# A cross-attention kernel on one core: new memory map of the opening, normalisation on ScalarE, Wo stores behind product stores

## The chip, the cores and the metric

The kernel runs on one core of a Trainium2 chip. The metric is the device time of one execution in microseconds (us); the time of a kernel is the median of its runs. Engines: PE is TensorE (matmuls), DVE is VectorE, ACT is ScalarE, POOL is GpSimd, SP is SyncE, which here issues all DMAs. SBUF has 128 partitions; addresses below are KiB within a partition. PSUM has eight banks of 128x512 f32.

## The reference

```python
a = layer_norm(ctx, gamma, beta)                 # ctx: 8 x 64 x 1024
Q = x @ Wq.T                                     # x: 8 x 1024 x 1024, 16 heads of 64
K = a @ Wk.T ; V = a @ Wv.T
attn = softmax(Q K^T / 8, masked)                # per head, 64 keys
out = x + tanh(gate) * (attn V) @ Wo.T
```

All in float32.

## The kernel before

**Algebra.** Scores are not made from Q. For each batch b the kernel first makes M[b] = Wq^T K[b]^T (1024 x 1024: model dimension by 16 heads x 64 keys), so that the scores of a batch are x[b] @ M[b]. The output is (attn V) @ Wo^T, so the main loop is 32 products of 512 x 1024 by 1024 x 1024: rounds n = 0 to 15 (scores, two a batch, with M[b]) and n = 16 to 31 (output, with Wo). Each product is made by Strassen's scheme in Winograd's form: seven half-size products, in the order P1, P5, P6, P3, P7, P2, P4. Every product of the seven is a step s = 7n + k (224 steps), of two items g = 0, 1, each four groups of three matmuls: every f32 operand is split into a high part (rounded to fp32r) and a low part, and high x high, high x low and low x high are summed. A step lasts 5.44 us on PE.

**Per step.** The left operand (a quarter of x, or a sum of quarters that `sum_a` makes in `a_sum`) is split by ACT (`split_a_hi`) and DVE (`split_a_lo`) into `a_ring`. The right operands are split once a batch into `parts` (seven regions of 16 KiB at 0 to 112) by `split_b_hi` on ACT and `split_b_lo` on DVE, in 14 half pieces q (q // 2 is the product, 0 = P1, 1 = P5, 2 = P6, 3 = P3, 4 = P7, 5 = P2, 6 = P4); `sum_b` (DVE) makes the sums in `b_raw` between them, counted by `t_made`. `refill_step` says behind which step a piece is split; -1 is ahead of step 0. P1, P5, P6 and P4 of a scores round are first uses and are copied out by ACT, the others are added to `c_out` by DVE (`add_out`), and `store_quad` stores them. PE's `item` waits for these splits, copies and adds. P5, P3 and P2 share two banks, so the P2 step waits for the add of P3.

**The opening.** SP loads four tiles of the context, the constants (gamma, beta, gate, mask, on one semaphore `consts_in`), 16 weight items (`load_weight`, 256 KB), then x. DVE takes statistics of each tile, POOL the reciprocal root (`rstd`), DVE normalises (L777), PE transposes (L1030), DVE scales by gamma and beta, ACT and DVE split. ACT splits the high part of a weight item (`split_weight_hi`, L622), POOL the low one (L574). Then PE makes 48 items in a written-out order (`OPS`): K in 16, M in 16 (`m_pair`), V in 16, with the M items interleaved with K and V. M item i (half, c) gives 128 rows of M for all batches: ACT and DVE copy alternate banks to `m_stage` (three buffers), `store_m` stores them. Batch 0's parts go directly to `b_raw` (L389, L391; the last four, on `b22_in`, are the second quadrant pair), the others to DRAM scratch. V is split in `v_out` and stored by `store_v`.

**Order.** Every engine works its own queue in program order, and SP its DMA queue. ACT ahead of step 0: weight splits, M copies, then `refills(-1)` (q 0 to 3), `split_a_hi(0)`, the four V splits. DVE: the same for its side, with `sum_b` behind each `split_b_lo`. SP: after all items it waits for `m_stored[1]` and `b22_in[1]`, since x pair 1 lies in a stage buffer, loads x(1), stores V, loads x(2); then `slot(z)` for each half step: product stores (`after_product`), x loads, Wo quarter loads, Wo stores, M loads, x quads and softmax loads.

**Wo.** During the first scores rounds the Wo matrix is read in quarters, summed (`sum_wo`), split (`round_wo` on ACT, `split_wo_lo` on DVE) into `wo_ring` of three slots, and stored to DRAM scratch in 56 pieces (`store_wo_split`, L364), to be loaded as `parts` later. ACT waits before a piece until the store of three pieces earlier has landed.

## Time and profile before

| | |
|---|---|
| median of 3 runs | 1564.25 us (1563.99 to 1564.56) |
| profiled execution, its time | 1560.93 us |
| its span (first to last instruction) | 1559.2 us |
| PE busy | 1531.3 us (98%), 7104 matmuls |
| DVE busy | 1128.9 us (72%) |
| ACT busy | 872.8 us (56%) |
| POOL busy | 356.1 us (23%) |
| DMA | 289.77 MB, mean 186 GB/s |
| chain that ended last | PE 90%, DMA 4%, DVE 3% |

Starts are us from the span's start. A PE record of 0.39 us is one 128x512 matmul in a pipeline: successive ones start 0.227 us apart. A timeline row is start, duration, engine, line, operation, output<-input, count, and in brackets how long the engine had been idle before it and what released it.

### The profile page before, as it was taken

Reading aid. Unit: us, or ns where it says so; the run is one execution under the profiler, and the core shown is the slowest. Engines: PE = TensorE matmul, PEld = TensorE weight load, DVE = VectorE, ACT = ScalarE, POOL = GpSimd, SP = SyncE. Lnnn points to the kernel's source line nnn. Section 1 sums busy time; section 2 is a strip of 40 time slices with the busy share of each in tenths; the row PEclk is TensorE's granted clock in tenths of the full one; section 3 lists DMA queues with packets and bytes.
Section 4 is the critical chain, followed back from the end, with each engine's and each line's share of the span. In section 5 each row is a group of like instructions: output and inputs, shape, how many; then the busy total and the mean of one; then the engine's idle time right before and its main releaser. Section 6 shows DMA issues by size and latency. Waiting matters only on the chain.

```text
span 1559.2 us, 20380 instructions
## 1 busy us (share of the span) xinstructions
PE 1531.3 (98%) x7104; PEld 1245.8 (80%) x7104; DVE 1128.9 (72%) x1356; ACT 872.8 (56%) x1874; POOL 356.1 (23%) x254
## 2 busy tenths in 40 slices
PE   7999899999999999999999999999999999999998
PEld 5666778888888888887887888888888888888887
DVE  6445888787878787879857777777777777777643
ACT  3556445454545454547766666666666666666521
POOL 5333000000000000001233344432344333444320
PEclk9999999999999999999999999999999999999999
DMA  7799765656565656556689344553445533445321
GB/s 251 222 364 392 275 215 178 210 202 222 178 220 187 211 182 216 190 188 184 202 292 294 115 136 142 157 157 114 125 125 168 169 123 120 123 145 167 109 93 69
DMA packets 225077, 289.77 MB, mean 186 GB/s; under 512 B 28240, under 2 KB 112336, under 8 KB 224976
## 3 DMA queue, kind: packets, MB, share of 16 engines
q1 hardware_dynamic: 224976, 288.48, 56.6%
q8 instruction: 57, 0.93, 0.2%
q14 instruction: 44, 0.36, 0.1%
HBM read 168.89 MB, written 116.39 MB: 183 GB/s over the span
## 4 chain that ended last, share of the span: by engine, by line
PE 90%; DMA 4%; DVE 3%; issue 1%; SPq 1%; ACT 0%; POOL 0%; DVEq 0%; ACTq 0%
PE banks L1036 28%; PE banks L1038 28%; PE banks L1037 28%; PE banks L1104 4%; PE banks L1065 3%; DMA wo_split_scratch<-wo_ring 1%; DMA xq<-x_t 1%; DMA m_scratch<-m_stage 1%; DVE parts L878 1%; DMA s_scratch<-c_out 1%; DVE a_sum L939 1%; DVE a_ring L872 1%; ACT a_ring L684 0%; PE banks L1160 0%; DMA c_out<-x 0%
## 5 line engine op out<-in xcount | busy, mean ns | idle before, releaser
L1036 PE MATMUL banks<-parts,a_ring 128*128 128x512 f32 x1792 | 711.6, 397 | 5.8 <-DVE a_ring L872 3.6
L1038 PE MATMUL banks<-parts,a_ring 128*128 128x512 f32 x1792 | 700.1, 391 | 0.0
L1037 PE MATMUL banks<-parts,a_ring 128*128 128x512 f32 x1792 | 698.9, 390 | 0.0
L1036 PEld LDWEIGHTS banks<-parts,a_ring 128*128 128x128 f32 x1792 | 336.9, 188 | 75.3 <-DVE a_ring L872 5.9
L1038 PEld LDWEIGHTS banks<-parts,a_ring 128*128 128x128 f32 x1792 | 336.8, 188 | 72.2
L1037 PEld LDWEIGHTS banks<-parts,a_ring 128*128 128x128 f32 x1792 | 337.4, 188 | 66.7
L961 DVE TENSOR_TENSOR c_out<-banks,c_out 128x1024 f32<-128x1024 f32 x160 | 195.5, 1222 | 147.9 <-PE banks L1038 142.6
L732 ACT ACTIVATE probs<-probs,neg_max 128x64 f32<-128x64 f32 x1024 | 259.1, 342 | 1.7 <-DVE neg_max L966 1.7
L684 ACT CAST a_ring<-a_sum 128x1024 fp32r<-128x1024 f32 x128 | 134.3, 1049 | 219.4 <-PE banks L1038 199.6
L597 POOL TENSOR_TENSOR probs<-probs,row_rec 128x512 f32<-128x512 f32 x128 | 134.5, 1051 | 479.7 <-DVE row_rec L975 479.7
L872 DVE TENSOR_TENSOR a_ring<-a_sum,a_ring 128x1024 fp32r<-128x1024 f32 x128 | 180.3, 1409 | 79.4 <-ACT a_ring L684 79.4
L684 ACT CAST a_ring<-xq 128x1024 fp32r<-128x1024 f32 x96 | 100.9, 1051 | 179.0 <-PE banks L1038 178.1
L872 DVE TENSOR_TENSOR a_ring<-xq,a_ring 128x1024 fp32r<-128x1024 f32 x96 | 117.9, 1228 | 52.1 <-ACT a_ring L684 52.1
L878 DVE TENSOR_TENSOR parts<-b_raw,parts 128x1024 fp32r<-128x1024 f32 x112 | 135.3, 1215 | 0.7 <-ACT parts L707 0.7
L607 POOL MEMSET v_diag<- 128x2048 f32 x1 | 1.8, 1821 | 566.8 <-DVE parts L878 566.8
L707 ACT CAST parts<-b_raw 128x1024 fp32r<-128x1024 f32 x112 | 114.1, 1048 | 9.6 <-DVE b_raw L898 5.2
L749 ACT COPY xq<-banks 128x512 f32<-128x512 f32 x128 | 75.2, 588 | 78.4 <-PE banks L1038 75.4
L979 DVE TENSOR_TENSOR p_parts<-banks,p_parts 128x512 fp32r<-128x512 f32 x128 | 86.2, 673 | 38.1 <-ACT p_parts L741 38.1
L741 ACT CAST p_parts<-banks 128x512 fp32r<-128x512 f32 x128 | 74.2, 580 | 67.1 <-PE banks L1104 66.8
L966 DVE TENSOR_REDUCE neg_max<-probs 128x8 f32<-128x512 f32 x128 | 83.7, 665 | 6.9 <-ACT probs L732 6.9
L844 DVE COPY m_stage<-banks 128x512 f32<-128x512 f32 x64 | 43.7, 690 | 60.4 <-PE banks L1065 48.0
L971 DVE TENSOR_REDUCE row_sum<-probs 128x8 f32<-128x512 f32 x128 | 86.4, 675 | 0.0
(75 smaller groups left out, 1354.4 us busy)
## 6 DMA issues: line engine op xcount, KB each, us to landing
xq<-x_t SPq DMA_DIRECT2D x32, 1024.0 KB, 6.8
s_scratch<-c_out SPq DMA_DIRECT2D x64, 512.0 KB, 3.1
probs<-s_scratch SPq DMA_DIRECT2D x128, 256.0 KB, 4.0
c_out<-x SPq DMA_DIRECT2D x64, 512.0 KB, 4.5
out<-c_out SPq DMA_DIRECT2D x64, 512.0 KB, 3.1
b_raw<-m_scratch SPq DMA_DIRECT2D x29, 1024.0 KB, 6.7
m_scratch<-m_stage SPq DMA_DIRECT2D x16, 1792.0 KB, 13.9
wo_split_scratch<-wo_ring SPq DMA_DIRECT2D x56, 256.0 KB, 5.7
```

The costliest lines, as they stand in the source:

```text
L597: nc.gpsimd.tensor_tensor(pr, pr, rec, ALU.mult).then_inc(probs_done, 1)
L684: nc.scalar.copy(a_ring[:, s % 2, 0], a_source(n, k)).then_inc(a_hi_made, 1)
L707: nc.scalar.copy(parts[:, k, 0, c:c + 2, :], b_raw[:, B_HOME[k], c:c + 2, :]).then_inc(b_hi_made, 1)
L732: last = nc.scalar.activation(prob(u)[:, cols], prob(u)[:, cols], ACT.Exp, bias=neg_max[:, u % 2, g:g + 1])
L872: nc.vector.tensor_tensor(a_ring[:, s % 2, 1], a_source(n, k), a_ring[:, s % 2, 0].bitcast(F32), ALU.subtract).then_inc(a_lo_made, 1)
L878: nc.vector.tensor_tensor(parts[:, k, 1, c:c + 2, :], b_raw[:, B_HOME[k], c:c + 2, :], parts[:, k, 0, c:c + 2, :].bitcast(F32), ALU.subtra ...
L961: nc.vector.tensor_tensor(c_out[:, q], bank_pair(n, k), c_out[:, q], ALU.add).then_inc(added, 1)
L971: nc.vector.reduce_sum(row_sum[:, u % 2, :], prob(u).rearrange("p (g s) -> p g s", s=S), AX.X).then_inc(sum_done, 1)
L979: nc.vector.tensor_tensor(p_parts[:, u % 2, 1, :], banks[:, 6, :], p_parts[:, u % 2, 0, :].bitcast(F32), ALU.subtract).then_inc(p_lo_made, 1)
L1036: pe.matmul(to, wl, mh, start=first, stop=False, skip_group_check=joined)
L1037: pe.matmul(to, wh, ml, start=False, stop=False, skip_group_check=joined)
L1038: return pe.matmul(to, wh, mh, start=False, stop=last, skip_group_check=joined)
```

## The change

- **Memory map of the opening.** `xq` moves from 144 to 136 and `a_sum` from 136 to 160, so that x pairs 0 and 1 lie outside the stage buffers (152 to 200), while `a_sum` and x pair 2 lie in one. `w_ring` moves to 48, `k_half` to 16 and 32, and `v_out` becomes two tensors, at 32 and at 96.
- **SP.** x(0) and x(1) are loaded behind the first 16 weights, x(2) where x(1) was. The V store of half 0 comes one M item earlier. The first context tile is loaded in two halves. Wo stores come directly behind `after_product`, ahead of x loads and quarter loads.
- **P1, P5, P6 ahead of step 0.** q 0 and 1 are split and the P5 sums made between the copies of M items 13 and 14; q 2 and 3 are split, the P6 sums made, `split_a(0)`, then q 4 and 5. The rest moves one step earlier (P3 behind step 1, P7 2, P2 3, P4 4). Two of the four V splits of DVE move behind `split_a_lo(1)`, and step 1 waits for two less.
- **Normalisation.** ACT normalises tiles 0 to 2 and the first half of tile 3 with `rstd` and `neg_mean`, a new product by DVE; DVE does the last half. ACT's queue begins with the wait for the constants and tanh, then tiles with weight splits between. POOL's low splits wait for `last_normed`.
- **End.** The last product is added and stored in two halves.

```diff
-        a_sum = at("a_sum", 136, [P, 2, HC, 2, P])
-        xq = at("xq", 144, [P, 3, HC, HT])
+        xq = at("xq", 136, [P, 3, HC, HT])
+        a_sum = at("a_sum", 160, [P, 2, HC, 2, P])
...
-        w_ring = at("w_ring", 16, [P, 8, 2, HD], F32R)
-        k_half = [at(f"k_half{h}", 48 + 16 * h, [P, 2, HC, B * S], F32R) for h in range(2)]
-        v_out = at("v_out", 48, [P, 2, CT, HD], F32R)
+        k_half = [at(f"k_half{h}", 32 - 16 * h, [P, 2, HC, B * S], F32R) for h in range(2)]
+        w_ring = at("w_ring", 48, [P, 8, 2, HD], F32R)
+        v_out = [at("v_out0", 32, [P, 2, CT, HD], F32R), at("v_out1", 96, [P, 2, CT, HD], F32R)]
...
-                return (-1, -1, -1, -1, 0, 0, 1, 1, 2, 2, 4, 4, 5, 5)[q]
+                return (-1, -1, -1, -1, -1, -1, 1, 1, 2, 2, 3, 3, 4, 4)[q]
...
-            for i in range(CT):
+                                 v_out[half][:, part].bitcast(F32)).then_inc(v_stored[half], 16)
+
+            sp.dma_start(ctx_n[:, 0, 0:HD], ctx_x[0:P, 0:HD]).then_inc(ctx_in[CT], 16)
+            sp.dma_start(ctx_n[:, 0, HD:D], ctx_x[0:P, HD:D]).then_inc(ctx_in[0], 16)
+            for i in range(1, CT):
...
             load_x(0)
+            load_x(1)
...
-                if (kind, half, c) == ("V", 1, 1):
+                if (kind, half, c) == ("V", 1, 0):
                     store_v(0)
             sp.wait_ge(m_stored[1], 32 * 4 + 16)
             sp.wait_ge(b22_in[1], 16)
-            load_x(1)
+            load_x(2)
             store_v(1)
-            load_x(2)
...
                 if g == 0:
+                    for w in wo_pieces(s - 1):
+                        store_wo_split(w)
...
-            after_product(2 * ROUNDS - 1, P4)
-            for s in q_stored:
-                sp.wait_ge(s, 16 * 2 * ROUNDS)
+            for g in range(2):
+                n, q = 2 * ROUNDS - 1, TARGET[P4]
+                sp.wait_ge(added, 3 * ROUNDS + 7 * ROUNDS - 1 + g + 1)
+                sp.dma_start(quad_rows(out, n, q)[:, g], c_out[:, q, g]).then_inc(q_stored[q], 16)
+            for q in range(4):
+                sp.wait_ge(q_stored[q], 16 * (2 * ROUNDS + (1 if q == TARGET[P4] else 0)))
...
-            pool.wait_ge(normed, CT)
+            pool.wait_ge(last_normed, 2)
...
+            def normalise_context(i):
+                act.wait_ge(neg_mean_made, i + 1)
+                n = D if i < CT - 1 else HD
+                nc.scalar.activation(ctx_n[:, i, 0:n], ctx_n[:, i, 0:n], ACT.Identity, bias=neg_mean[:, i:i + 1],
+                                     scale=rstd[:, i:i + 1]).then_inc(normed if i < CT - 1 else last_normed, 1)
+
             def split_ctx_hi(c):
                 act.wait_ge(a_scaled, c + 1)
                 nc.scalar.copy(a_parts[:, 0, c, :], a_scaled_t[:, c, :]).then_inc(ctx_hi_made, 1)
@@ -646,31 +660,20 @@
                 if i == 0 and half == 0:
                     act.wait_ge(mask_step, 7)
                 if i == 0 and half == 1:
-                    act.wait_ge(v_stored[0], 32)
-                nc.scalar.activation(v_out[:, 0, i, :], banks[:, 4 + i, :], ACT.Copy,
+                    act.wait_ge(v_done, 2 * CT)
+                nc.scalar.activation(v_out[half][:, 0, i, :], banks[:, 4 + i, :], ACT.Copy,
                                      scale=v_scale[:, i:i + 1]).then_inc(v_hi_made, 1)
 
-            for w in range(3):
-                split_weight_hi(w)
             act.wait_ge(consts_in, 64)
             nc.scalar.activation(tanh_gate[:], gate_s[:], ACT.Tanh).then_inc(gate_ready, 1)
+            for i in range(CT):
+                normalise_context(i)
+                if i > 0:
+                    split_weight_hi(i - 1)
             for c in range(NC):
                 split_ctx_hi(c)
...
+                    act.wait_ge(m_done, 4 * GROUPS)
+                elif rnd == 0 and q == 4:
+                    act.wait_ge(v_stored[0], 32)
+                elif rnd == 0 and q == 6:
                     for w in range(40, 44):
                         wait_item_used(act, w)
-                elif rnd == 0 and q == 4:
+                elif rnd == 0 and q == 8:
                     act.wait_ge(v_done, 2 * CT)
-                elif rnd == 0 and q == 6:
+                elif rnd == 0 and q == 12:
...
-            for rnd, q in refills(-1):
-                split_b_hi(rnd, q)
+            for t in range(ITEMS):
+                kind, half, c = OPS[t]
+                if t + LEAD < ITEMS:
+                    split_weight_hi(t + LEAD)
+                if kind == "M":
+                    for p in range(4):
+                        copy_m(NC * half + c, p)
+                        if (half, c) == (1, 5) and p % 2 == 1:
+                            split_b_hi(0, p // 2)
+                elif c == NC - 1 and kind == "K":
+                    copy_k_hi(half)
+                elif c == NC - 1 and half == 0:
+                    for i in range(CT):
+                        copy_v_hi(0, i)
+
+            for q in range(2, 4):
+                split_b_hi(0, q)
             split_a_hi(0)
+            for q in range(4, 6):
+                split_b_hi(0, q)
             for i in range(CT):
                 copy_v_hi(1, i)
...
+            def take_stats(i, h):
+                dve.wait_ge(ctx_in[CT if i == 0 and h == 0 else i], 16)
+                nc.vector.bn_stats(stats[:, i, h, :], ctx_n[:, i, h * 512:(h + 1) * 512]).then_inc(stats_made, 1)
+
+            def take_neg_mean(i):
                 dve.wait_ge(rstd_made, i + 1)
-                nc.vector.tensor_scalar(ctx_n[:, i, :], ctx_n[:, i, :], mean_var[:, i, 0:1], rstd[:, i:i + 1],
-                                        ALU.subtract, ALU.mult).then_inc(normed, 1)
+                nc.vector.scalar_tensor_tensor(out=neg_mean[:, i:i + 1], in0=mean_var[:, i, 0:1], scalar=-1.0,
+                                               in1=rstd[:, i:i + 1], op0=ALU.mult, op1=ALU.mult
+                                               ).then_inc(neg_mean_made, 1)
 
             for i in range(CT):
-                dve.wait_ge(ctx_in[i], 16)
-                for h in range(2):
-                    nc.vector.bn_stats(stats[:, i, h, :], ctx_n[:, i, h * 512:(h + 1) * 512]).then_inc(stats_made, 1)
+                take_stats(i, 0)
+                take_stats(i, 1)
                 dve.wait_ge(stats_made, 2 * i + 2)
                 nc.vector.bn_aggr(mean_var[:, i, :], stats[:, i, :, :]).then_inc(mean_made, 1)
                 dve.wait_ge(mean_made, i + 1)
                 nc.vector.tensor_scalar(var_eps[:, i:i + 1], mean_var[:, i, 1:2], EPS, None, ALU.add
                                         ).then_inc(var_added, 1)
                 if i > 0:
-                    normalise_context(i - 1)
-            normalise_context(CT - 1)
+                    take_neg_mean(i - 1)
+            take_neg_mean(CT - 1)
+            last = ctx_n[:, CT - 1, HD:D]
+            nc.vector.tensor_scalar(last, last, mean_var[:, CT - 1, 0:1], rstd[:, CT - 1:CT],
+                                    ALU.subtract, ALU.mult).then_inc(last_normed, 1)
...
-                    if q // 2 in (0, 1, 2, 5):
+                    if q // 2 in (0, 1, 2, 5) and (rnd > 0 or q // 2 == 5):
...
+            def add_last(g):
+                n, q = 2 * ROUNDS - 1, TARGET[P4]
+                dve.wait_ge(item_done, 2 * (STEPS - 1) + g + 1)
+                if g == 0:
+                    dve.wait_ge(q_in[q], 16 * (n - ROUNDS + 1))
+                    dve.wait_ge(added, 3 * ROUNDS + 7 * (n - ROUNDS) + P4)
+                nc.vector.tensor_tensor(c_out[:, q, g], bank_pair(n, P4)[:, g], c_out[:, q, g], ALU.add
+                                        ).then_inc(added, 1)
...
+                        if (half, c) == (1, 5) and p % 2 == 1:
+                            split_b_lo(0, p // 2)
+                        if (half, c) == (1, 6) and p % 2 == 1:
+                            sum_b(0, P5, p // 2)
...
+            for q in range(2, 4):
+                split_b_lo(0, q)
+            for h in range(2):
+                sum_b(0, P6, h)
             split_a_lo(0)
+            for q in range(4, 6):
+                split_b_lo(0, q)
             sum_a(0, P5)
-            for i in range(CT):
+            for i in range(2):
                 split_v_lo(1, i)
             for s in range(STEPS):
                 n, k = s // 7, s % 7
@@ -993,9 +1046,15 @@
                     add_out((s - 1) // 7, (s - 1) % 7)
                 if s + 1 < STEPS:
                     split_a_lo(s + 1)
+                if s == 0:
+                    for i in range(2, CT):
+                        split_v_lo(1, i)
                 if n < ROUNDS:
                     if k == P1:
                         sum_a(n, P6)
+                    if s == 0:
+                        for h in range(2):
+                            sum_b(0, P7, h)
...
-                        pe.wait_ge(v_lo_made, 2 * CT)
+                        pe.wait_ge(v_lo_made, CT + 2)
```

## Rows read from the trace of the kernel before

**Rows 1.** Who PE waited for: us in total, times, longest.
```profile
PE banks L1030 <- DVE ctx_n L777: 9.4, 4, 8.5
```

**Rows 2.** Timeline of the opening, several engines.
```profile
4.12 0.46 SPq L406 DMA_DIRECT2D mask_u<-mask  x1
...
8.47 1.94 PE L1030 MATMUL banks<-ident,ctx_n 128*128 128x128 f32 x8 [8.47 <-DVE ctx_n L777]
...
12.29 1.98 ACT L622 CAST w_ring<-w_raw 128x512 fp32r<-128x512 f32 x3 [10.28 <-DMA w_raw<-wk_t]
...
13.46 0.81 DVE L777 TENSOR_SCALAR ctx_n<-ctx_n,mean_var,rstd 128x1024 f32<-128x1024 f32 x1 [0.44 <-POOL rstd L566]
...
14.33 1.09 PE L1030 MATMUL banks<-ident,ctx_n 128*128 128x128 f32 x8 [0.16 <-DVE ctx_n L777]
...
17.55 0.47 PE L1036 MATMUL banks<-a_parts,w_ring 128*128 128x512 f32 x1 [2.13 <-DVE a_parts L800]
```

**Rows 3.** DMA issues at 4.1: count, KB, us from issue to landing.
```profile
mask_u<-mask SPq DMA_DIRECT2D x1, 64.0 KB, 7.5
```

**Rows 4.** ACT: line view (ns min/median/max) and costliest groups (busy us, mean ns).
```profile
L650 ACT ACTIVATE v_out<-banks,v_scale x8: 678/687/690, 127.0 to 165.3; 128x512 fp32r<-128x512 f32 x8
...
L684 ACT CAST a_ring<-a_sum 128x1024 fp32r<-128x1024 f32 x128 | 134.3, 1049 | 219.4 <-PE banks L1038 199.6
...
L741 ACT CAST p_parts<-banks 128x512 fp32r<-128x512 f32 x128 | 74.2, 580 | 67.1 <-PE banks L1104 66.8
```

**Rows 5.** PE's timeline at steps 0, 2, 5; one window (PE, PEld, ... PEclk, DMA).
```profile
168.28 0.50 PE L1160 MATMUL banks<-mask_mov,ones_row 128*128 128x512 f32 x1 [2.99 <-DVE a_ring L872]
...
170.14 0.63 PE L1038 MATMUL banks<-parts,a_ring 128*128 128x512 f32 x1
...
183.03 0.50 PE L1036 MATMUL banks<-parts,a_ring 128*128 128x512 f32 x1 [1.03 <-DVE a_ring L872]
...
201.43 0.47 PE L1036 MATMUL banks<-parts,a_ring 128*128 128x512 f32 x1 [1.79 <-issue]
...
170.00:171.00 1.00, 1.00 (x4) 0.72 (x4) 0.00 (x0) 0.00 (x0) 0.00 (x0) 0.50 0.12 45
```

**Rows 6.** DVE's timeline ahead of step 0 and behind it.
```profile
163.38 1.23 DVE L898 TENSOR_TENSOR b_raw<-b_raw 128x1024 f32<-128x1024 f32 x1 [1.62 <-DMA b_raw<-m_stage]
...
167.01 1.22 DVE L872 TENSOR_TENSOR a_ring<-xq,a_ring 128x1024 fp32r<-128x1024 f32 x1
171.17 1.23 DVE L939 TENSOR_TENSOR a_sum<-xq 128x1024 f32<-128x1024 f32 x1 [2.94 <-DMA xq<-x_t]
```

**Rows 7.** DVE's timeline ahead of step 5.
```profile
200.11 1.22 DVE L878 TENSOR_TENSOR parts<-b_raw,parts 128x1024 fp32r<-128x1024 f32 x1
```

**Rows 8.** DMA issues between 186.5 and 188.5.
```profile
b_raw<-m_scratch SPq DMA_DIRECT2D x1, 1024.0 KB, 5.0
```

**Rows 9.** The M products: timeline of ACT, DVE, PE; one window (last: DMA share, GB/s).
```profile
139.50 1.28 ACT L641 COPY m_stage<-banks 128x512 f32<-128x512 f32 x2 [1.89 <-PE banks L1065]
...
136.33 1.38 DVE L844 COPY m_stage<-banks 128x512 f32<-128x512 f32 x2 [1.78 <-PE banks L1065]
...
138.50 1.66 PE L1065 MATMUL banks<-k_half,w_ring 64*128 64x512 f32 x12
...
80.00:165.00 85.00, 82.96 (x450) 57.58 (x450) 43.17 (x59) 47.09 (x81) 29.20 (x23) 1.00 1.05 381
```

**Rows 10.** First Wo round: ACT's and PE's timeline; DMA issues at 289.5 to 290.2.
```profile
297.56 0.41 ACT L714 CAST wo_ring<-wo_quarter 128x256 fp32r<-128x256 f32 x1 [4.74 <-DMA wo_split_scratch<-wo_ring]
...
307.43 0.50 PE L1036 MATMUL banks<-parts,a_ring 128*128 128x512 f32 x1 [0.60 <-DVE a_ring L872]
...
wo_split_scratch<-wo_ring SPq DMA_DIRECT2D x1, 256.0 KB, 7.7
```

**Rows 11.** The end: DVE's last instruction, and the last DMA issue.
```profile
1554.62 1.22 DVE L961 TENSOR_TENSOR c_out<-banks,c_out 128x1024 f32<-128x1024 f32 x1 [4.21 <-PE banks L1038]
...
out<-c_out SPq DMA_DIRECT2D x1, 512.0 KB, 2.8
```

More of the change, by code:

```diff
@@ L116, in xattn_kernel @@
         gate_ready = sem("gate_ready")
-        ctx_in = sems("ctx_in", CT)
+        ctx_in = sems("ctx_in", CT + 1)
         stats_made = sem("stats_made")
@@ L505, in slot @@
                             load_wo_quarter(i)
-                    for w in wo_pieces(s - 1):
-                        store_wo_split(w)
                     for rnd, q in refills(s - 1):
@@ L828, in _, with make_mask @@
                                         ).then_inc(mask_step, 1)
+            def make_mask(rnd):
+                wait(dve, item_done, 2 * (14 * (rnd - 1) + 8))
+                src = mask_u8[0:1, rnd:rnd + 1, :].to_broadcast([1, NC, S])
+                nc.vector.tensor_scalar(mask_mov[0:1], src, -1.0, BIG, ALU.add, ALU.mult).then_inc(mask_made, 1)
+            nc.vector.memset(mask_mov[:].bitcast(F32), 0.0).then_inc(rows_zeroed, 1)
+            dve.wait_ge(rows_zeroed, 3)
+            make_mask(0)
             def split_k_lo(half):
@@ L848, in split_v_lo @@
                 dve.wait_ge(v_hi_made, CT * half + i + 1)
-                nc.vector.scalar_tensor_tensor(out=v_out[:, 1, i, :], in0=banks[:, 4 + i, :],
-                                               scalar=v_scale[:, i:i + 1], in1=v_out[:, 0, i, :].bitcast(F32),
+                nc.vector.scalar_tensor_tensor(out=v_out[half][:, 1, i, :], in0=banks[:, 4 + i, :],
+                                               scalar=v_scale[:, i:i + 1], in1=v_out[half][:, 0, i, :].bitcast(F32),
                                                op0=ALU.mult, op1=ALU.subtract).then_inc(v_lo_made, 1)
-            for t in range(ITEMS):
-                kind, half, c = OPS[t]
-                if kind == "M":
-                    for p in range(4):
-                        copy_m(NC * half + c, p)
-                elif c == NC - 1 and kind == "K":
-                    split_k_lo(half)
-                elif c == NC - 1 and half == 0:
-                    for i in range(CT):
-                        split_v_lo(0, i)
-            def make_mask(rnd):
-                wait(dve, item_done, 2 * (14 * (rnd - 1) + 8))
-                src = mask_u8[0:1, rnd:rnd + 1, :].to_broadcast([1, NC, S])
-                nc.vector.tensor_scalar(mask_mov[0:1], src, -1.0, BIG, ALU.add, ALU.mult).then_inc(mask_made, 1)
             def split_a_lo(s):
@@ L928, in sum_a @@
                         dve.wait_ge(a_lo_made, 7 * (n - 1) + P3 + 1)
+                    else:
+                        dve.wait_ge(m_stored[1], 32 * 4 + 16)
+                        dve.wait_ge(b22_in[1], 16)
                 elif k == P6:
@@ L1021, in _ @@
                     make_mask(s // 14 + 1)
-            add_out(2 * ROUNDS - 1, P4)
+            for g in range(2):
+                add_last(g)
         @block.tensor
@@ L1027, in _ @@
             for i in range(CT):
-                pe.wait_ge(normed, i + 1)
+                if i < CT - 1:
+                    pe.wait_ge(normed, i + 1)
+                else:
+                    pe.wait_ge(last_normed, 2)
                 for c in range(NC):
```

33 lines of the change are left out of this document (14 added, 19 removed).

## Prediction

> **What bounds the kernel now.** I read the page first: TensorE (PE) is busy 98% of the span, and the chain that ended last lies 90% on it. So the order of reading is: list what PE waited for, find each wait in the timeline, and ask what released it. Only these places can be bought. Back-to-back 128x512 matmuls start 0.227 us apart; each longer pause is a stall. PE's pauses in order of time: the opening, where it first works at 8.47 and starts its matmul stream at 17.55 [rows 1, 2]; 3.1 us lost between the last V product and step 0 of the main loop, after which the granted clock shows the lower level (1.2 GHz) for 3.4 us, matmuls start 0.427 apart, and some 1.6 us more are lost; 1.2 us ahead of step 2; 1.95 ahead of step 5 [rows 5]; 0.3 each ahead of steps 1 and 6. Later 0.8, 1.0, 1.3 and 1.0 us near 307, 540, 740 and 821 (the first stands in [rows 10]), and behind the last matmul the tail of 4.6 us. All else is matmuls in a row.
>
> **The opening.** Today VectorE (DVE) normalises: 0.80 us a tile, the last ending at 14.27, then PE transposes the last tile from 14.33 and the stream begins 3.22 us later [rows 2]. The change moves three and a half of four tiles to ScalarE (ACT). DVE gains: a tile costs it two bn_stats, an aggregate, an add and one tiny product, about 1.85 us where it was 2.35. Its own last half tile would be done near 13.2.
> But what stands ahead of the ACT work? Its queue now begins with the wait for all four constants (consts_in 64), then tanh, and only then tile 0. The mask's load is issued at 4.12 and lands 7.5 us later, at 11.6 [rows 2, 3]. Today this wait is free, as it stands behind the three weight splits, whose first byte lands late too: they start at 12.29. In the new order it holds every tile. With one more load ahead of it I put the constants at 11.8.
> Price of an ACT tile: a 128x1024 cast takes 1.05 us; of two 128x512 operations out of the banks, the one with a scale read from a tile takes 0.687 and the plain cast 0.580, so such an operand adds 0.107, and two of them make a tile 1.26 (0.83 for the half), about 0.1 of which overlaps the next [rows 4]. The bounds are 1.05 and 1.26; I take the latter.
> ACT: tanh to 11.95, tile 0 to 13.2, tile 1 to 14.35, first weight split, tile 2 to 16.1, second split, half of tile 3 to 17.4.
> PE: the first eight transposes took 1.94 us at 8.47, the last eight 1.09 [rows 2]; the fast ones come some 4 us after PE's first work. Started at 13.25, tiles 0 and 1 take 3.7 at the slow rate, tile 2 about 1.0, so tile 3 starts at 17.95 instead of 14.33: **+3.6 us**. The chain behind (scale, split, first matmul) is unchanged, and the POOL splits, which wait for the same tile, have more than 3 us of room. Bounds: +2.1 (ACT at the cheaper price, PE no limit) and +4.6 (all transposes slow).
> A rule of the Trainium skill speaks against this part (ScalarE: Activation LUTs, "Rules for kernel authors"): multiply and add belong on VectorE. The trace agrees on the rate, 0.80 us on DVE against 1.05 for a mere cast on ACT. By that page's own price (0.28 us plus 0.833 ns an element) a tile would be an estimated 1.13 and the sum would be 0.3 us better.
>
> **The K, M and V products** shift as a block. The second x load goes into the slack after 16 us and pushes weight 16, not needed before about 60, back by 2.6 us. Into the M products go two ACT casts, two DVE splits and two DVE sums (P1, P5). After each pair of copies (1.28 and 1.38 us) ACT is free 1.89 and DVE 1.78 us, and PE wants the bank back at 138.50 where the copies end at 137.71 [rows 9]. A cast and its split in a row take 2.27, so the next copies slip by 0.4 to 0.5, inside the 0.8 of room: cost 0. Room gone, each of the two would cost 0.5. The earlier V store only changes places with other stores.
>
> **The transition, in today's times.** The DMA engines are full from 60 to 165 (share 1.05) [rows 9], so the last direct block of M lands at 163.1, and the first sum for P6 waits for it: DVE idles 1.62 and starts at 163.38. Behind it in DVE's queue stand a split, a sum and then the split that step 0 needs, 167.01 to 168.24 [rows 6]. In the new order P1, P5 are split long before, and between block and step 0 stand two sums: 163.38, 164.52, the split 165.65 to 166.88. Step 0 starts at 166.95 instead of 168.28: **-1.35**. The pause shrinks from 3.0 to 1.7 us. At 199.25 PE paused 1.8 us without a fall of its clock, so I take the lower level as gone: **-1.6**. The Trainium skill (TensorE: Matmul & The Clock Gate, "What's actually happening") also has the clock fall for idleness alone; by it too the new sum stands.
> Today DVE then idles 2.94 us for x [rows 6]. In the new order x is there. Counting on at DVE's pitch of 1.13 (0.66 for a V split): two P6 splits to 169.1, sum P5 to 170.3, two V splits, split for step 1 to 172.75, when step 0 ends at 173.0: **-0.3**, no stall. Two V splits, sum P6, two P7 sums, split for step 2 to 178.6; step 1 ends at 178.45: 0.2 lost of 1.2 today: **-1.0**. Step 2 waits for nothing else, and steps 3 and 4 have over 1 us.
> Step 5 today waits for the second P2 split, 200.11 to 201.33 [rows 5, 7]. In the new order P2 is split at step 3, but its block is loaded only when P3 is split, at 182.1, and lands 5.0 us later [rows 8], at 187.1. Then cast to 188.2, split, sum, split, sum to 193.2, the split for step 5 to 194.4, and the add of P3, on which step 5 waits, to 195.5, where step 4 ends at 195.1: 0.45 lost instead of 1.95: **-1.5**, from 0 (load as late as 188.5) to -1.95. Step 6 has its parts: **-0.3**. Together **-6.2**, from -4.3 to -6.8.
> ACT waits for the V store and for free weight slots in these steps; both are past by then.
>
> **Wo stores.** Stores now stand ahead of x and quarter loads in SP's queue. SP waits for the Wo splits up to 3.5 us at a time; x loads have 7 steps or no Wo piece ahead of them, quarter loads wait for the same splits anyhow, and the M loads stood behind the stores already: cost 0. The gain: two of three waits of ACT shorten. But the stall near 307 hangs on the third: ACT waits 4.74 us for a store issued at 289.74 directly behind the product store already, which lands 7.7 us later because an M load and other stores are ahead of it on the DMA rings [rows 10]. Its place stays. **0**; bounds -2.2 (both stalls near 307 and 540 gone with their restart) and +0.5.
>
> **The end.** Now a 1.22 us add from 1554.62 and a 512 KB store, 2.8 us to landing [rows 11]. New: half an add (0.69, the 128x512 copy out of the banks [rows 9]) and half a store; 256 KB less at 400 GB/s is 0.65. The first half is done during PE's last item. **-1.2**, from -0.9 to -1.3.
>
> **Sum.** +3.6 - 6.2 + 0 - 1.2 = -3.8 us: span 1559.2 to 1555.4. The profiled execution took 1560.93, 1.7 above its span, and would take 1557.1; the three timed runs lie 3.3 higher, at 1564.25, so the forecast for the median is **1560.4**. About 0.2% (3.1 us) is what a measurement of this kernel can tell from no change.
>
> **Rivals.**
> (a) The constants don't hold ACT (they land by 8). Then the weight split behind tile 1 does (12.29 today), tile 3 starts at 15.0, opening +0.7: total -6.7, 1557.5. Against it: the 7.5 us of the mask. 0.15.
> (b) The transition gives half: the clock falls all the same (+1.6) and step 5 still waits (+1.5). Total -0.7, 1563.5. For it: the step 5 sum hangs on a landing to within 1.4 us. 0.20.
> (c) The Wo stalls go too: -6.0, 1558.2. Against: the third wait. 0.08.
> (d) Slower: the work put into the M products doesn't overlap with the idle time beside it and holds the banks. Twice 2.27 and twice 1.22 is up to 7.0 us; total +3.2, 1567.4. It decides once a slip exceeds the 0.8 of room. For it: this order of one cast and one split in a row exceeds the idle time. 0.10.
> (e) The memory map changes but neither end nor opening shows it: each part is a separate wait that the profile names, so I give this nothing of its own.
> The forecast itself has 0.47.
>
> **Chances.** Faster by over 0.2% (below 1561.1): two thirds of the forecast (0.32), (a), (c): 0.55. Within 0.2%: the rest of the forecast (0.15), (b), a little of (d): 0.37. Slower: 0.08. Range: the sum of the good ends is 2.1 - 6.8 - 2.2 - 1.3 = -8.2 and of the bad ones 4.6 - 4.3 + 0.5 - 0.9 = -0.1; as not all fall together, and with (b) and part of (d) inside, 1557.0 to 1564.6.
>
> **What the new profile would show.** tanh waits for the constants near 11.8, the transposes start near 13 and the stream near 21.2; step 0 starts 1.3 us nearer to the last V matmul, with no clock row at 0.5 behind it; DVE runs without idling from the last direct block to step 2; step 5 loses under 1 us; the stall in the first Wo round is still there; the last add is 0.69. Wrong would be: a stream that starts before 19, stalls of PE inside the M products at 135 to 150, or a low clock behind the transition.

## The result and the profile after

The changed kernel takes 1558.35 us (median of 7 runs, 1557.34 to 1560.98), the kernel before 1564.25 (7 runs, 1562.8 to 1566.82). The ratio is 0.9967 (95% interval 0.9958 to 0.9976), that is 5.2 us or 0.33% less; the medians themselves lie 5.9 us apart. The forecast was 1560.4, 3.8 us less. Two executions in the experiment on Wo stores (1921 and 6367 us) and one in that on half of P6 (4776 us) were disturbed, and no comparison below uses them. The profiled execution took 1558.14 with a span of 1556.4, 2.8 below the span of the first profile of before.

| us | before | after |
|---|---|---|
| span of the profile | 1559.2 | 1556.4 |
| first transpose, first matmul of the stream | 8.47, 17.55 | 14.68, 23.04 |
| last V matmul | 164.91 | 171.05 |
| step 0, step 6 start | 168.28, 207.30 | 172.85, 207.07 |
| last V matmul to step 6 | 42.39 | 36.02 |
| step 6 to the last matmul | 1346.89 | 1345.61 |
| last matmul to the end of the span | 5.0 | 3.7 |

The table is made from the first and last matmul records of each stretch in PE's timeline. It says at once what happened: the opening became 5.5 us longer, the stretch from there to the last V matmul 0.65 longer, the transition 6.4 shorter, the rest 1.3 and the end 1.3 shorter.

PE's waits in the profile after (us in total, times, longest), where before had [rows 1]:

```profile
PE banks L1093 <- ACT ctx_n L635: 14.7, 1, 14.7
PE banks L1099 <- DVE a_parts L831: 2.6, 1, 2.6
...
PE banks L1128 <- DVE m_stage L884: 1.8, 2, 0.9
PE banks L1223 <- DVE a_ring L896: 1.4, 1, 1.4
```

PE now waits 14.7 us for the first tile that ACT normalises. Why, the timeline of the opening shows, against [rows 2]:

```profile
8.18 1.28 DVE L801 BATCH_NORM_STATS2 stats<-ctx_n 128x6 f32<-128x512 f32 x2 [2.36 <-DMA ctx_n<-ctx_x]
...
13.20 0.20 ACT L668 ACTIVATE tanh_gate<-gate_s 128x1 f32<-128x1 f32 x1 [11.19 <-DMA mask_u<-mask]
...
13.31 2.36 ACT L635 ACTIVATE ctx_n<-ctx_n,neg_mean,rstd 128x1024 f32<-128x1024 f32 x2
...
14.68 5.78 PE L1093 MATMUL banks<-ident,ctx_n 128*128 128x128 f32 x32 [14.68 <-ACT ctx_n L635]
...
17.74 0.81 ACT L635 ACTIVATE ctx_n<-ctx_n,neg_mean,rstd 128x512 f32<-128x512 f32 x1
...
21.31 1.58 DVE L831 TENSOR_TENSOR a_parts<-a_scaled_t,a_parts 128x512 fp32r<-128x512 f32 x1
...
23.04 0.47 PE L1099 MATMUL banks<-a_parts,w_ring 128*128 128x512 f32 x1 [2.58 <-DVE a_parts L831]
```

ACT stood idle 11.19 us in front of tanh, for the mask's load, and only then took tiles 0 and 1. The `neg_mean` of tile 0 had been ready since 9.96. The first line holds a second delay, looked for by no one: DVE waited 2.36 us for the second context tile. The fourth line shows what follows: PE's 32 transposes run without a pause, so from 14.68 to 20.46 PE itself is the limit, and ACT's last half tile (fifth line) is done at 18.55, in time. The sixth line is DVE's low split of the first context slice, for which the stream waits; in the kernel before it took 1.13:

```profile
16.27 1.13 DVE L800 TENSOR_TENSOR a_parts<-a_scaled_t,a_parts 128x512 fp32r<-128x512 f32 x1
```

The transition, PE and DVE, against [rows 5, 6]:

```profile
171.05 0.39 PE L1101 MATMUL banks<-w_ring,a_parts 128*128 128x512 f32 x1
172.85 0.51 PE L1223 MATMUL banks<-mask_mov,ones_row 128*128 128x512 f32 x1 [1.41 <-DVE a_ring L896]
```

```profile
169.29 2.36 DVE L922 TENSOR_TENSOR b_raw<-b_raw 128x1024 f32<-128x1024 f32 x2 [5.57 <-DMA b_raw<-m_stage]
171.57 1.22 DVE L896 TENSOR_TENSOR a_ring<-xq,a_ring 128x1024 fp32r<-128x1024 f32 x1
...
174.98 1.22 DVE L966 TENSOR_TENSOR a_sum<-xq 128x1024 f32<-128x1024 f32 x1
176.12 1.40 DVE L889 SCALAR_TENSOR_TENSOR v_out<-banks,v_scale,v_out 128x512 fp32r<-128x512 f32 x2
177.44 1.21 DVE L896 TENSOR_TENSOR a_ring<-a_sum,a_ring 128x1024 fp32r<-128x1024 f32 x1
```

Between the direct block and the split for step 0 stand two sums, and behind the split DVE does not idle: the P5 sum, which waited 2.94 us for x in [rows 6], starts as its turn comes. The granted clock stays at the higher level (the window of 173 to 174 us; columns as in [rows 5]):

```profile
173.00:174.00 1.00, 1.00 (x5) 0.81 (x6) 1.00 (x2) 1.00 (x3) 0.00 (x0) 1.00 0.77 293
```

The end, DVE's last two instructions and the last DMA issue, against [rows 11]:

```profile
1550.38 0.69 DVE L996 TENSOR_TENSOR c_out<-banks,c_out 128x512 f32<-128x512 f32 x1 [1.50 <-PE banks L1101]
1553.11 0.69 DVE L996 TENSOR_TENSOR c_out<-banks,c_out 128x512 f32<-128x512 f32 x1 [2.03 <-PE banks L1101]
```

```profile
out<-c_out SPq DMA_DIRECT2D x1, 256.0 KB, 2.0
```

0.53 less for the add, 0.8 less for the store.

### The profile page after: what moved, and what is told of

Same layout as the page of the kernel before. It is cut to its first block, busy times and chain, and to the rows that moved or that the text cites. A ratio compares the mean times of both kernels' runs of the same rounds, so it can differ in the third digit from the quotient of the medians.

```text
span 1556.4 us, 20392 instructions
## 1 busy us (share of the span) xinstructions
PE 1528.3 (98%) x7104; PEld 1246.5 (80%) x7104; DVE 1126.5 (72%) x1358; ACT 876.8 (56%) x1878; POOL 356.6 (23%) x254
## 4 chain that ended last, share of the span: by engine, by line
PE 90%; DMA 4%; DVE 3%; issue 1%; SPq 1%; ACT 1%; POOL 0%; DVEq 0%; ACTq 0%
PE banks L1099 28%; PE banks L1101 28%; PE banks L1100 28%; PE banks L1167 4%; PE banks L1128 3%; DMA m_scratch<-m_stage 1%; DVE parts L902 1%; DMA b_raw<-m_stage 1%; DVE a_ring L896 1%; DMA s_scratch<-c_out 1%; DMA wo_split_scratch<-wo_ring 1%; DMA mask_u<-mask 1%; DVE a_sum L966 0%; DVE b_raw L922 0%; PE banks L1223 0%
## 5 line engine op out<-in xcount | busy, mean ns | idle before, releaser
L922 DVE TENSOR_TENSOR b_raw<-b_raw 128x1024 f32<-128x1024 f32 x64 | 78.1, 1224 | 10.1 <-DMA b_raw<-m_stage 5.6
```

## The experiments

All but the first are the changed kernel with one thing edited; the last two join findings. The labels e0 to e9 stand in the headings. "Stretch" below is the time from the last V matmul to step 6, and "stream" the start of the first 128x512 matmul, both read from PE's timeline. How far one profile can be trusted, the kernels that share a part show: the six with the transition as changed (the changed kernel and e1 to e5) have stretches of 35.9 to 36.5, but the six with the opening as changed (the changed kernel and e5 to e9) have streams at 21.3 to 23.2. The runs' medians scatter by 1 to 2 us, and the intervals of e1 to e4, e9 and the joined kernels all overlap that of the changed kernel.

### The kernel before once more (e0)

> The kernel before, unchanged, for a second profile of it: the first one took 1560.9 us where its other runs took 1561.6 to 1566.8. Theory A (its usual execution has what the profiled one happened to lack): the lower clock level comes once more behind the start of the stream, or the stream starts 1 us or more later than 17.55, which together make up to 3 us; its time is 1562 to 1565. Rival B (the difference lies around the span, not in it): the span is within 0.5 us of 1559.2. From the last V matmul to step 6 it takes 42.4 us as in the first profile, to 0.5, with the lower level behind the pause of 3 us.

Measured: 1564.5 us, span 1562.7 (3.5 above the first profile). The windows show what the first profile lacked:

```profile
18.00:19.00 1.00, 1.00 (x3) 0.81 (x4) 1.00 (x2) 0.61 (x1) 0.77 (x1) 0.50 1.06 389
19.00:20.00 1.00, 1.00 (x3) 0.77 (x3) 1.00 (x3) 0.90 (x3) 0.00 (x0) 0.50 1.05 385
20.00:21.00 1.00, 1.00 (x4) 0.75 (x3) 1.00 (x2) 0.82 (x2) 0.67 (x1) 0.50 1.04 381
...
172.00:173.00 1.00, 1.00 (x4) 0.71 (x4) 0.00 (x0) 0.00 (x0) 0.00 (x0) 0.50 0.11 43
```

The stream began at 17.78, and with it 3.4 us at the lower level; the last V matmul came at 167.00 instead of 164.91. The stretch is 42.76 (42.39), with the lower level again behind the pause ahead of step 0. Theory A holds: the profile on which the forecast rested lacked one fall of the clock that this one has, and some 2 us of the gap between it and the median lie in the opening, 1.1 in the later steps. The other executions bear it out: the mean granted clock is 0.999 in the first profile and 0.997 in this one, and in 26 further executions of the kernel before it is 0.996 to 0.998 in 25 and 0.999 in one, the shortest of them (1561.59 us). The changed kernel has 0.999 or 1.000 in all seven. So the first profile was an uncommonly good execution of the kernel before (no other is below its 1560.93 us), and that is much of why the runs moved by 5.2 us where the two first profiles differ by 2.8.

### Constants behind the tiles (e1)

```diff
-            act.wait_ge(consts_in, 64)
-            nc.scalar.activation(tanh_gate[:], gate_s[:], ACT.Tanh).then_inc(gate_ready, 1)
             for i in range(CT):
                 normalise_context(i)
                 if i > 0:
                     split_weight_hi(i - 1)
+            act.wait_ge(consts_in, 64)
+            nc.scalar.activation(tanh_gate[:], gate_s[:], ACT.Tanh).then_inc(gate_ready, 1)
```

> The changed kernel with ScalarE's wait for the four constants, and tanh, moved behind the four tiles and the three weight splits; nothing else. Theory A (the constants hold the tiles; behind them the weight loads do, as a weight split stands between tiles 1 and 2): tile 0 is normalised as soon as its mean is there (8 to 10 us), tile 2 only behind the first weight split (weight landed 12.2 to 13.9), the matmul stream starts near 20.3 instead of 23.04, the span falls by 2.7 us. Rival B (the price of the opening is ScalarE's rate and TensorE's slow transposes, not the wait): the stream starts within 0.5 us of 23.0.

Measured: ratio to before 0.9950 (0.9935 to 0.9965), span 1555.2, stream at 20.14. ACT's timeline:

```profile
11.28 1.24 ACT L635 ACTIVATE ctx_n<-ctx_n,neg_mean,rstd 128x1024 f32<-128x1024 f32 x1 [0.46 <-DVE neg_mean L805]
13.88 0.62 ACT L630 CAST w_ring<-w_raw 128x512 fp32r<-128x512 f32 x1 [1.35 <-DMA w_raw<-wk_t]
14.40 1.24 ACT L635 ACTIVATE ctx_n<-ctx_n,neg_mean,rstd 128x1024 f32<-128x1024 f32 x1
```

Theory A: the stream starts 2.9 us earlier than in the changed kernel's profile, and behind the constants the first weight's landing is the next gate, with a ready tile queued behind the split. Since kernels with the same opening start their stream anywhere from 21.34 to 23.17, the gain of the move is 1.2 to 3.0; steadier is the first transpose, at 10.97 where all six have 14.2 to 14.8. Only 1.2 us of the 2.9 show in the span, because this execution had the lower clock level at 21.4 to 24.8, as the kernel before had in its second profile.

### Tiles first (e2)

The same, with the three weight splits behind all four tiles too.

> The changed kernel with ScalarE's queue reordered: four tiles, then three weight splits, then the wait for the constants and tanh. Theory A: nothing but VectorE's statistics holds the tiles, so the last half tile is done at 13.0 to 15.0 and the stream starts at 16.3 to 18.2, the span falls by 4.8 to 6.7 us, and the kernel is about as fast in the opening as the kernel before or 1 us faster. Rival B (ScalarE is the wrong engine: 1.2 us a tile where VectorE took 0.8): the stream starts 1 us or more behind the 17.55 of the kernel before even when the tiles land as early as there.

Measured: ratio 0.9953 (0.9938 to 0.9968), span 1554.4, stream at 18.56, last V matmul at 166.98, 4.1 us earlier than in the changed kernel. Now ACT waits only for DVE:

```profile
12.76 1.95 ACT L635 ACTIVATE ctx_n<-ctx_n,neg_mean,rstd 128x1024 f32<-128x1024 f32 x2 [0.46 <-DVE neg_mean L805]
14.61 1.64 ACT L630 CAST w_ring<-w_raw 128x512 fp32r<-128x512 f32 x3
```

The stream started 0.4 us later than expected at most, and 1 us behind 17.55, with the late second tile, so that the condition of Rival B (tiles that land as early as before) wasn't given and it stays undecided. ACT's rate no longer holds the tiles: it idles 0.45 us in front of tiles 1 and 2. What does is DVE's queue, where the `neg_mean` of tile 0 stands behind the statistics of the late tile 1 (its `rstd` was there at 5.94, ACT began at 9.37), and then PE, whose 32 transposes run from 10.75 to 16.49 without a pause. Computing the first `neg_mean` ahead of those statistics was not tried.

### VectorE normalises again (e3)

> The changed kernel with the opening of the kernel before (VectorE normalises, ScalarE's queue begins with three weight splits, the first tile is loaded whole). Theory: the stream starts at 17.5 as before, all the rest of the change stands, so the span is 5.5 us below the changed kernel's 1556.4, near 1551, and the ratio to the kernel before is near 0.994. If the later stalls absorbed part of the late opening, less than 5 us comes back.

The edit puts back the opening of the kernel before; all else stays changed. Measured: ratio 0.9950 (0.9931 to 0.9969), span 1554.9, stream at 18.91, last V matmul 168.95, with the lower clock level at 20.1 to 23.5. Of the 5.5 us expected, 4.1 came back in the stream, 2.1 at the last V matmul, 1.5 in the span. A miss in size. The stream is 1.4 later than before: 0.75 because PE's transposes, which began at 8.61, ran 0.213 us apart to the end, where in [rows 2] the later ones were twice as fast, and 0.6 because DVE's first low split took 1.75 instead of 1.13. The fall of the clock behind the stream's start takes 1.6 more, and step 6 to the last matmul takes 0.5 more than in the changed kernel's profile.

### First tile whole (e4)

```diff
-            sp.dma_start(ctx_n[:, 0, 0:HD], ctx_x[0:P, 0:HD]).then_inc(ctx_in[CT], 16)
-            sp.dma_start(ctx_n[:, 0, HD:D], ctx_x[0:P, HD:D]).then_inc(ctx_in[0], 16)
-            for i in range(1, CT):
+            for i in range(CT):
```

> The changed kernel with the first context tile loaded by one DMA of 512 KB again. In the changed kernel the second tile landed at 8.2 (5.4 before) and the constants at 13.2 (11.6 before). Theory A (the two 256 KB loads with their 2 KB rows, and the one more DMA ahead, are the cause): tile 1 lands near 5.5, the constants near 11.7, the stream starts near 21.6, 1.4 us earlier. Rival B (the slowest DMA engine's lag differs from one execution to the next): the landings move by chance and no steady gain shows beside the other kernels of this call.

Measured: ratio 0.9960 (0.9945 to 0.9975), span 1558.7. The constants are there 1.5 us earlier, DVE and ACT:

```profile
6.06 1.28 DVE L799 BATCH_NORM_STATS2 stats<-ctx_n 128x6 f32<-128x512 f32 x2
```

```profile
11.70 0.20 ACT L666 ACTIVATE tanh_gate<-gate_s 128x1 f32<-128x1 f32 x1 [9.68 <-DMA mask_u<-mask]
```

That is no chance: tile 1's statistics start at 7.55 to 8.35 in all nine profiles with the first tile in halves, and at 5.9 to 6.2 in the five that load it whole (both profiles of before, e3, e4 and the other joined kernel); the six kernels with halves and the early wait have tanh at 12.7 to 13.3. So theory A holds for the landings. Most of the delay of the constants is one of issue: SP issued the mask's load at 5.0 to 5.6 with halves and at 4.1 to 4.3 without. The stream, though, starts at 21.54, where the kernels with halves have 21.3 to 23.2: the transposes began at 13.18, but ran 0.213 us apart for 5.1 us, until 18.3, and 0.109 apart only then. Landings are shown; a gain in time is not.

### Wo stores back (e5)

```diff
                 if g == 0:
-                    for w in wo_pieces(s - 1):
-                        store_wo_split(w)
                     y = 2 * (n + 1)
...
                             load_wo_quarter(i)
+                    for w in wo_pieces(s - 1):
+                        store_wo_split(w)
```

> The changed kernel with the Wo stores back behind the x and quarter loads. Theory A (the prediction's: the moved stores don't reach the piece that the stall hangs on): stalls of 0.7 to 1.5 us near 307 as before and after, the one near 540 comes and goes by itself (it was absent in three of five profiles with the new order), time within 1 us of the changed kernel. Rival B (the store order took the stall near 540 away): both stalls are there, 1 to 1.5 us each, and the time is 1 to 2.5 us longer.

Measured: 1560.4 and 1560.8 us in two executions (before: 1563.4), some 2 us above the changed kernel's median where I had expected 1 at most. In the profile this excess lies ahead of the Wo rounds (from stream to last V matmul 150.24 instead of 148.01, with the lower clock level at 23.0 to 26.4); from step 6 to the last matmul it takes 1345.54 instead of 1345.61. Stalls: 0.35 near 307, less than expected, and 0.54 near 540. ACT's waits for the ring, here and in the changed kernel:

```profile
291.07 0.41 ACT L721 CAST wo_ring<-wo_sum 128x256 fp32r<-128x256 f32 x1 [3.35 <-DMA wo_split_scratch<-wo_ring]
...
299.10 0.41 ACT L721 CAST wo_ring<-wo_quarter 128x256 fp32r<-128x256 f32 x1 [4.65 <-DMA wo_split_scratch<-wo_ring]
```

```profile
286.52 0.41 ACT L721 CAST wo_ring<-wo_sum 128x256 fp32r<-128x256 f32 x1 [1.08 <-DMA wo_split_scratch<-wo_ring]
...
297.53 0.41 ACT L721 CAST wo_ring<-wo_quarter 128x256 fp32r<-128x256 f32 x1 [5.74 <-DMA wo_split_scratch<-wo_ring]
```

The new order shortens the first wait (1.08 instead of 3.35 us), and the third stays: it ends at 297.53 in the changed kernel where it ended at 297.56 before [rows 10]. That is the prediction's reading. The stall near 540 was 1.0 and 1.65 us in the two profiles of before, and in the eleven with the new order 0 in five and 0.36 to 1.84 in six. So no effect of the order shows; what makes that stall come and go was not found.

### x late (e6)

```diff
             load_x(0)
-            load_x(1)
...
-            load_x(2)
+            load_x(1)
             store_v(1)
+            load_x(2)
```

> The changed kernel with the second x pair loaded behind the last stage store and the third behind the V store, as before. Theory A (x is the one thing that idles VectorE behind step 0): the load lands some 15 us after its issue, at about 178 where step 0 starts at 173, VectorE idles about 3 us ahead of the P5 sum, step 1 starts 2.5 to 3.5 us late, and step 6 starts some 3 us later than in the changed kernel. Rival B (the early splits alone carry the gain, with x early or late): step 6 starts within 0.7 us of the changed kernel, counted from the last V matmul.

Measured: 1564.4 us in a single execution, as slow as the kernel before; span 1562.6, stretch 41.43 instead of 36.02. DVE:

```profile
173.87 2.35 DVE L902 TENSOR_TENSOR parts<-b_raw,parts 128x1024 fp32r<-128x1024 f32 x2
177.90 1.23 DVE L966 TENSOR_TENSOR a_sum<-xq 128x1024 f32<-128x1024 f32 x1 [1.68 <-issue]
```

DVE idles 1.7 us, half of what I expected, since the load landed 13.3 us after its issue and two P6 splits cover a part. But the cost is larger than expected: 1.8 us are lost ahead of step 1 (0.3 in the changed kernel), and 2.5 ahead of step 5 (0.5), whose M load lands 7.1 us after its issue instead of 5.0; behind that pause of 2.4 us the clock fell once more (207 to 210.4), another 1.6. Without the falls the stretch is 40.8 before, 39.8 here, 36.0 in the changed kernel. So with the new order of splits in place, the early x loads (both pairs are moved) carry 3.8 of the 4.8 us. What they would give with the old order was not run, so the two shares need not add up the other way round.

### Splits behind the M products (e7)

The two P1 splits and the P5 sums go from between the M copies to behind them, on ACT and DVE.

> The changed kernel with P1's two splits and the P5 sums taken out of the M products and put behind them, ahead of the P5 splits. In the changed kernel VectorE idles 5.6 us there for the last direct block of M, and what is moved in takes some 4.8 us. Theory A (that idle time would have held them): step 0 starts 1.8 us behind the last V matmul as now, from there to step 6 it takes 36.0 us to 0.3, nothing is lost. Rival B (the placement between the M copies is needed): step 0 starts 0.5 to 2 us later.

Measured: stretch 35.97, step 0 starts 1.79 behind the last V matmul (1.80), span 1557.0. DVE:

```profile
164.37 2.36 DVE L900 TENSOR_TENSOR parts<-b_raw,parts 128x1024 fp32r<-128x1024 f32 x2
167.63 2.36 DVE L920 TENSOR_TENSOR b_raw<-b_raw 128x1024 f32<-128x1024 f32 x2 [0.90 <-DMA b_raw<-m_stage]
169.91 1.22 DVE L894 TENSOR_TENSOR a_ring<-xq,a_ring 128x1024 fp32r<-128x1024 f32 x1
```

Theory A: the idle time of 5.6 us takes them all and 0.9 is left. Placing this work between the M copies cost nothing, as forecast (stream to last V matmul 148.05 without it, 148.01 with it), and gained nothing.

### Step 0 later (e8)

```diff
-            split_a_lo(0)
             for q in range(4, 6):
                 split_b_lo(0, q)
+            split_a_lo(0)
```

> The changed kernel with VectorE's split for step 0 behind the two low splits of P6. Step 0 starts 2.3 us later, so TensorE pauses 3.7 us where it paused 1.4. Theory A (the fall of the clock in the kernel before came of its 3 us pause): the granted clock shows the lower level for 3.4 us soon behind the pause and 1.6 us more are lost; from the last V matmul to step 6 it takes 3 to 4 us longer. Rival B (the fall was chance, whatever the pause): no lower level there, and the stretch is 1.6 to 2.3 us longer.

Measured: 1561.4 us, stretch 38.96. PE's timeline and the windows behind it:

```profile
173.54 0.50 PE L1223 MATMUL banks<-mask_mov,ones_row 128*128 128x512 f32 x1 [3.67 <-DVE a_ring L896]
```

```profile
174.00:175.00 1.00, 1.00 (x6) 0.76 (x5) 1.00 (x2) 0.34 (x1) 0.00 (x0) 0.80 0.17 68
175.00:176.00 1.00, 1.00 (x4) 0.81 (x3) 1.00 (x3) 0.71 (x1) 0.00 (x0) 0.50 0.02 6
```

A pause of 3.67 us brings the lower level back a microsecond behind it. Ahead of step 0 the pauses were 2.66 and 2.99 (before), 3.67 here, each with a fall, and 1.4 in the eight kernels that kept this pause, none with one. Theory A. The stretch is 2.94 longer, at the edge of what was expected, as steps 1 to 5 lose 0.9 less once step 0 starts late.

### Half of P6 early (e9)

```diff
-            for h in range(2):
-                sum_b(0, P6, h)
-            split_a_lo(0)
-            for q in range(4, 6):
-                split_b_lo(0, q)
+            sum_b(0, P6, 0)
+            split_b_lo(0, 4)
+            split_a_lo(0)
+            sum_b(0, P6, 1)
+            split_b_lo(0, 5)
```

The first half's sum waits for direct blocks 0 and 1 alone.

> The changed kernel in which the first half of the P6 sum waits for its own two direct blocks of M alone, and it and the first P6 split stand ahead of the split for step 0, the second half behind it. Theory A (step 0 hangs on the last direct block only by way of VectorE's queue): the split for step 0 is done before the last V matmul, the pause of 1.4 us is gone, steps 1 and 2 lose 0.3 to 0.5 each, and from the last V matmul to step 6 it takes 0.8 to 1.2 us less. Rival B (VectorE's work as a whole is the limit of the first steps): the pause moves to steps 1 and 2 and less than 0.3 us is gained.

Measured: stretch 34.97, 1.05 less; PE goes from V to step 0 without a pause (169.53 to 169.76), and loses 0.75 and 0.42 ahead of steps 1 and 2. DVE:

```profile
167.83 1.23 DVE L895 TENSOR_TENSOR a_ring<-xq,a_ring 128x1024 fp32r<-128x1024 f32 x1 [2.08 <-ACT a_ring L687]
168.97 1.22 DVE L925 TENSOR_TENSOR b_raw<-b_raw 128x1024 f32<-128x1024 f32 x1
```

Theory A: the last direct block held step 0 only through DVE's queue. The ratio to before is 0.9972 (0.9960 to 0.9983), no better than the changed kernel's: step 6 to the last matmul took 3.2 us more than in that kernel's profile, with stalls of 1.7 near 540 and 1.9 near 820. A gain of 1 us is shown for the stretch, not for the whole.

### Both in one kernel

> Both findings in one kernel: the changed kernel with ScalarE's queue as tiles, weight splits, constants, and with the first half of the P6 sum ahead of the split for step 0. Expected from the two single runs: stream near 18.5 instead of 22 to 23, from the last V matmul to step 6 35.0 us instead of 36.0; 2 to 3 us below the changed kernel, ratio to the kernel before 0.994 to 0.9955. If the M products, whose stores fill the DMA engines, set the pace, the earlier stream comes back as stalls near 118 and 126, and about 2 us of it is lost there.

Measured: 1555.84 us (1554.94 to 1557.41), ratio 0.9949 (0.9936 to 0.9961), span 1553.2. Stream at 18.80, last V matmul 166.11, stretch 34.87. That is 8.0 us below the kernel before. The changed kernel's 0.9967 lies outside this interval, but its own (0.9958 to 0.9976) overlaps it, and e1, e2 and e3 alone had 0.9950 to 0.9953: the profile shows both parts, while the time does not show that joining them gained anything over the better queue alone. The stalls in the M products did not take the gain: stream to last V matmul is 147.3.

> The same with the opening of the kernel before (VectorE normalises, ScalarE begins with the weight splits, first tile whole) instead of the reordered queue. If ScalarE's price for a tile matters, this one starts its stream 1 us earlier than the other (17.5 to 18.5) and is up to 1 us faster; otherwise the two are equal to 0.1%.

Measured: 1557.03 us, ratio 0.9957 (0.9944 to 0.9971), span 1552.1, stream at 17.85, stretch 35.53. The stream starts 0.95 us earlier, as expected of ACT's price and the late tile together (the pair does not separate them, and a stream's start scatters by more), but this profile had the lower level at 19.3 to 22.7, the other had not. In time the two can't be told apart.

## Why the prediction was right

**The opening** (+3.6 forecast, +5.5 measured, above the stated bound of +4.6). The mechanism was right and its size too small. ACT stood idle for the constants and then ran the tiles in the queue's order, each at 1.24 us (forecast 1.26). Mis-sized was the landing of the constants: 13.2 instead of 11.8, because the first tile's halves were costed at nothing but one issue; e4, with the tile whole, has them at 11.7. That is 1.4 of the 1.9 us. The transposes took what I had added up for them, 5.78 us against 3.7 + 1.0 + 1.09. The other 0.45 is the chain behind them, which I had called unchanged: from the last transpose to the stream 2.58 instead of 2.13, as DVE's low split took 1.58 us instead of 1.13. That split scattered from 0.80 to 1.75 over the fourteen profiles; why, no run shows. The other source of scatter is the point at which the transposes go from 0.213 to 0.109 us apart: 4.3 us after the first one here, 3.9 in the first profile of before, 2.7 to 4.8 in the other five kernels with this opening, whose streams start at 21.3 to 23.2, or +3.8 to +5.6. (The windows read 1.00 over both rates.)

**K, M and V products** (0, measured +0.65). No stall at the inserted splits, and e7 shows that they cost nothing. PE idles 0.9 us each near 121 and 129, where it idled 0.5 and 0.6. From stream to last V matmul all kernels without a fall of the clock take 147.3 to 148.4, those with one 149.0 to 150.2: it follows the stream and absorbs nothing.

**The transition** (-6.2, measured -6.4). Step 0 starts 1.80 behind the last V matmul (forecast 2.04), the clock stays up, step 5 loses 0.48 (forecast 0.45, with the load's 5.0 us). Here the row-by-row count of DVE's queue held to 0.3 us over 14 instructions. Rival (b), which needed the clock to fall all the same, didn't come: no fall stands behind the pause of 1.4 us in any of the eight kernels that have it, and e8, with 3.67, has one.

**Wo stores** (0). The third wait stayed, at the same time. The stall near 540 was absent in this profile (1.5 us with what follows from it in the next steps), which e5 doesn't tie to the change.

**The end** (-1.2, measured -1.3).

**The sum** is +5.5 + 0.65 - 6.4 - 1.3 - 1.3 = -2.8 in the profiles. The median moved by more, as the first profile of before lacked the fall behind the start of the stream: e0, with it, has a span of 1562.7. Had I taken the 3.3 us between profile and median as a sign that a typical execution carries one more fall of the clock, the late opening would have been compared with a less perfect one. Step by step, the 1.3 us behind step 6 lie at two places: the stall near 540 gives back 1.5, the one near 307 takes 0.2 more, and all other steps are equal to 0.1. Over all fourteen profiles this part varied between 1345.3 and 1348.8, by the stalls near 307, 540 and 820.

That the median came out within 2.1 us of the forecast is in part luck. The opening and the products were 2.5 us worse than the sum had them; a stall that comes and goes gave back 1.3 of that in the profile, and typical executions of the kernel before lose more to the clock than the profile that I had added up from, which more than made up for the rest. What was foreseen with its reasons is the transition, the third Wo wait, the end, and that the constants would hold ACT.

Rival (a) was wrong in its condition (the constants came late), and e1 shows that the weight split behind tile 1 would then have been the gate, as it said. Rival (d) didn't come.

## What to carry to other kernels

When an operation moves to another engine, read that engine's queue from its first instruction: a wait that cost nothing where it stood holds everything placed behind it. Here two lines, moved, let TensorE begin over 3 us earlier. And ask which transfer idles the engine on which the next stage waits: taking the early x loads away again cost 3.8 of the 4.8 us that the reordered stage had gained. And set the profile's own time against the median before you add up a forecast: the profile may be a better execution than most.

## What the runs showed of the hardware

- Loading the first of four tiles as two transfers of 256 KB let its statistics begin at 3.4 to 3.5 us instead of 4.3 to 4.6, those of the second tile at 7.6 to 8.4 instead of 5.9 to 6.2, and made the constants land 1.0 to 1.6 us later (12.7 to 13.3 in six profiles, 11.7 in e4).
- Around the start of the stream the granted clock fell to the lower level (1.2 GHz) for 3.4 us in seven of fourteen profiles and not in the others. The pause in front of it was 2.0 to 2.4 us in the seven and 1.8 to 2.6 in the others, so its length does not tell them apart; a fall cost about 1.6 us. At step 0 a fall followed each of the three pauses of 2.66 to 3.67 us, and at step 5 the one of 2.4 us (x late), but not those of 1.8 in the kernel before. What decides it the runs don't show.
- An ACTIVATE with scale and bias both read from tiles took 1.24 us on 128x1024 and 0.81 on 128x512, against 1.05 and 0.60 for a cast. The Trainium skill (ScalarE: Activation LUTs, "What ACT_TABLE_LOAD costs") has about 0.28 us plus 0.833 ns an element for one such operand and 0.09 more for each further one, which makes an estimated 1.23 for two on 128x1024; the trace agrees.
